# Softplus in a selective scan: in three of eight rounds one plus the exponential is made by ScalarE, and VectorE adds the positive part before the correction

## The reference

```
proj = u @ x_proj_w                                   # u: 2048 x 384
dt   = softplus(proj[..., :12] @ dt_w + dt_b)         # for each of two directions
B, C = proj[..., 12:28], proj[..., 28:]
h    = exp(dt * A) * h + (dt * u) * B                 # over the tokens, 16 states a channel
y    = sum over the states of h * C
```

## Time and profile before

| | us |
|---|---|
| median of 3 runs | 908.35 (907.75 to 909.34) |
| the profiled execution | 906.87 |
| its span on the core | 905.1 |

### The profile page before, as it was taken

The page is one execution under the profiler, slowest core; times in us unless marked ns, Lnnn a source line. Parts: engine busy times, 40 slices in busy tenths (PEclk is TensorE's granted clock), DMA queues, the critical chain, the costliest instruction groups (busy, mean ns, idle before and its releaser), DMA issues.

```text
span 905.1 us, 16651 instructions
## 1 busy us (share of the span) xinstructions
PE 779.2 (86%) x6060; PEld 705.2 (78%) x6061; DVE 733.4 (81%) x874; ACT 645.0 (71%) x1258; POOL 534.6 (59%) x343
## 2 busy tenths in 40 slices
PE   0389776899998999989999899995966899999990
PEld 0133335899998999989999899995955899999990
DVE  3788899889999899998999999998949455555554
ACT  0365879999999999989999999991331444444421
POOL 6430003799997999969999799893000344444420
PEclk9999989999999999999999999997955899999996
DMA  5003103265574764644746567377350111111106
GB/s 87 3 35 106 9 27 119 65 160 176 125 199 148 175 216 121 173 157 122 199 120 161 175 159 194 127 152 247 109 197 8 41 43 43 43 43 43 43 23 217
DMA packets 46453, 104.43 MB, mean 115 GB/s; under 512 B 16448, under 2 KB 25176, under 8 KB 46392
## 3 DMA queue, kind: packets, MB, share of 16 engines
q1 hardware_dynamic: 35784, 74.67, 25.5%
q0 software_dynamic: 8352, 27.07, 15.0%
q10 hardware_dynamic: 2256, 1.87, 0.6%
HBM read 83.77 MB, written 19.82 MB: 114 GB/s over the span
## 4 chain that ended last, share of the span: by engine, by line
PE 47%; DVE 22%; ACT 17%; POOL 7%; issue 4%; DMA 2%; DVEq 0%; ACTq 0%; POOLq 0%; SPq 0%
PE ps L1434 15%; PE ps L1738 8%; PE ps L1556 8%; DVE arena L836 8%; ACT arena L1261 6%; PE ps L1721 6%; POOL arena L623 5%; ACT arena L1244 5%; PE ps L1726 4%; ACT arena L1247 3%; PE ps L1454 3%; PE ps L1457 1%; DVE stats L670 1%; DVE arena L793 1%; DVE arena L802 1%
## 5 line engine op out<-in xcount | busy, mean ns | idle before, releaser
L623 POOL TENSOR_TENSOR arena<-arena 128x1024 f32<-128x1024 f32 x192 | 395.1, 2283 | 121.2 <-DVE arena L836 117.8
L836 DVE TENSOR_TENSOR_SCAN arena<-arena,ps 128x1024 f32<-128x1024 f32 x192 | 426.3, 2277 | 21.3 <-PE ps L1556 16.9
L1434 PE MATMUL ps<-ident,arena 128*128 128x128 f32 (+3 forms) x2622 | 347.2, 279 | 80.4 <-ACT arena L1124 37.4
L1434 PEld LDWEIGHTS ps<-ident,arena 128*128 128x128 f32 (+3 forms) x2622 | 298.1, 143 | 101.5 <-issue 52.9
L1261 ACT ACTIVATE arena<-arena,neg_a 128x510 f32<-128x510 f32 x384 | 241.0, 708 | 0.1
L627 POOL DMA_INDIRECT arena<-x_rows,arena x39 | 37.7, 967 | 160.5 <-DVE arena L1020 79.7
L1556 PE MATMUL ps<-arena,ln_in 128*128 128x128 f32 x768 | 104.0, 280 | 0.0
L1556 PE MATMUL ps<-arena 128*128 128x128 f32 x768 | 101.4, 275 | 0.0
L1556 PEld LDWEIGHTS ps<-arena,ln_in 128*128 128x128 f32 x768 | 95.9, 196 | 0.0
L1556 PEld LDWEIGHTS ps<-arena 128*128 128x128 f32 x768 | 93.3, 192 | 0.0
L1738 PE MATMUL ps<-arena,ln_in 128*128 x468 | 82.7, 327 | 0.8 <-DVE arena L1051 0.8
(11 more groups left out here) (217 smaller groups left out, 883.7 us busy)
## 6 DMA issues: line engine op xcount, KB each, us to landing
arena<-b_rows SPq DMA_DIRECT2D x64, 512.0 KB, 3.8
arena<-ws SPq DMA_DIRECT2D x16, 576.0 KB, 6.1
arena<-wf POOLq DMA_DIRECT2D x16, 576.0 KB, 7.9
arena<-hf POOLq DMA_DIRECT2D x16, 576.0 KB, 7.4
summed_first<-arena SPq DMA_DIRECT2D x8, 576.0 KB, 5.4
summed_second<-arena SPq DMA_DIRECT2D x8, 576.0 KB, 7.7
arena<-summed_second SPq DMA_DIRECT2D x8, 576.0 KB, 5.9
gates_dram<-arena SPq DMA_DIRECT2D x4, 768.0 KB, 3.4
```

The costliest lines, as they stand in the source:

```text
L623: g_.tensor_tensor(state[i % STATES], state[i % STATES], c_bc[u % C_BUFS], ALU.mult).then_inc(s_mul, 1)
L836: v.tensor_tensor_scan(o, a, x, 0.0, ALU.mult, ALU.add).then_inc(s_scan, 1)
L1434: return mm(o, src, ident[at:at + parts, at:at + parts], start=start, stop=True, is_transpose=True, skip_group_check=True)
```

## The change

In rounds 1, 3 and 5 ACT makes w = 1 + e, with a new instruction (Identity with a bias of 1, 128x1536) right behind the logarithm, and sets a new semaphore `s_w`; DVE leaves its own addition out there. In the same rounds DVE takes the positive part first (it waits for `s_l`), then the correction (it waits for `s_e` and `s_w`), then the subtraction. Rounds 0, 2, 4, 6 and 7 are as before. The function `pos_log` is cut in two, `add_pos` and `subtract_correction`.

```diff
--- before.py
+++ after.py
@@ -333,6 +333,7 @@
         s_e = sem("softplus_exp_ready")
         s_c = sem("softplus_corr_ready")
         s_pl = sem("softplus_pos_and_log_added")
+        s_w = sem("softplus_one_plus_exp_ready")
         s_l = sem("softplus_log_ready")
         s_lb_ps = sem("dt_and_b_product")
         s_lb = sem("dt_and_b_rows_ready")
@@ -418,6 +419,7 @@
         s_passed = sem("waits_passed")
         FRONT_LOADS, PAR_LOADS = 2, 34
         DT_BANK = 2
+        BY_ACT = (1, 3, 5)
         FIRST_BANKS = (0, 0, 0, 1, 0, 1, 0, 1)
 
         c_rows = b_rows
@@ -789,10 +791,13 @@
 
                 w, e = sp_w[n % SP], sp_e[n % SP]
                 dve.wait_ge(s_e, n + 1)
-                st.then(v.tensor_scalar(w, e, 1.0, None, ALU.add))
+                if n in BY_ACT:
+                    dve.wait_ge(s_w, BY_ACT.index(n) + 1)
+                else:
+                    st.then(v.tensor_scalar(w, e, 1.0, None, ALU.add))
                 v.scalar_tensor_tensor(w, w, -1.0, e, ALU.add, ALU.subtract).then_inc(s_c, 1)
 
-            def pos_log(n):
+            def add_pos(n):
 
                 g, d = divmod(n, 2)
                 dt = dt_all[g][d]
@@ -800,6 +805,10 @@
                 bank = ps[:, DT_BANK + DB * d:DT_BANK + DB * (d + 1), :].rearrange("p a b -> p (a b)")
                 flat = dt.rearrange("p a b -> p (a b)")
                 v.scalar_tensor_tensor(flat, bank, 0.0, flat, ALU.max, ALU.add).then_inc(s_pl, 1)
+
+            def subtract_correction(n):
+                g, d = divmod(n, 2)
+                dt = dt_all[g][d]
                 dve.wait_ge(s_pl, n + 1)
                 dve.wait_ge(s_c, n + 1)
                 v.tensor_tensor(dt, dt, sp_w[n % SP], ALU.subtract).then_inc(s_dt, 1)
@@ -808,12 +817,18 @@
                 v.tensor_tensor(dtu_b if d else dtu, dt_all[0][d], u_all[0], ALU.mult).then_inc(s_dtu, 1)
 
             for n in range(2 * NG):
-                correction(n)
+                if n in BY_ACT:
+                    add_pos(n)
+                    correction(n)
+                else:
+                    correction(n)
                 if n == 0:
                     dve.wait_ge(s_rset, 1)
                     st.then(v.tensor_copy(gain_1[:], ps[:, 1, 0:E]))
                     v.tensor_copy(w_route_sb[:, :, E + DR + 1:RC], ps[0:KC, 1, E:(1 + KT) * E].rearrange("p (k e) -> p k e", k=KT)).then_inc(s_wr, 1)
-                pos_log(n)
+                if n not in BY_ACT:
+                    add_pos(n)
+                subtract_correction(n)
                 if n in (4, 5):
                     dve.wait_ge(s_dt, n - 3)
                     times_u(n - 4)
@@ -1223,6 +1238,8 @@
                             keep_first_dtu_t(1)
                     act.wait_ge(s_e, n + 1)
                     a.activation(dt, sp_e[n % SP], ACT.Ln, bias=1.0).then_inc(s_l, 1)
+                    if n in BY_ACT:
+                        a.activation(sp_w[n % SP], sp_e[n % SP], ACT.Identity, bias=1.0).then_inc(s_w, 1)
                     if d == 0 and g + 1 < NG:
                         keep_lb(g + 1)
                     elif d == 0:
```

## The result

Measured with the prediction: 903.16 us (median of 4, 902.70 to 904.36) against 908.85 (median of 4, 907.75 to 909.37), ratio 0.9946 with a 95% interval of 0.9934 to 0.9958. I had forecast 904.6, 3.8 less than before; the medians differ by 5.7. Two more comparisons of the same two kernels gave 0.9971 (0.9961 to 0.9980) and 0.9964 (0.9950 to 0.9977), so 0.29% and 0.36% after 0.54%. The forecast of 904.6 thus lies 1.4 above the first median. By that comparison's 5.7 us the result falls into the case to which I had given 0.02 (more than 4.6); by the 3.0 and 3.5 us of the two later ones it falls into the second and the first case.

A forecast was written before the change was run, and what follows sets the result against it. Two engines in a row bound the softplus stage: DVE releases PE's banks, PE feeds ACT, ACT starts the loop. DVE's end 2.64 us and ACT 4.3 earlier start the loop 3.8 earlier: 908.35 - 3.8 = 904.6 us, range 902.9 to 907.2.

The forecast's parts named there:

- the case to which I had given 0.02: Whole kernel: an advance of more than 4.6 us, chance 0.02.
- the second and the first case: Second: only DVE's addition cut arrives, advance 1.6 to 3.3 us, chance 0.22; first: advance 3.3 to 4.6, chance 0.56.
- DVE's own cut: DVE's softplus stage: three additions fewer, less a new wait of 0.3 in round 1, end it 2.64 us earlier.
- The bank of round 5 free 4.32 earlier: DVE's positive part of round 5, moved to the front, ends at 126.94 instead of 131.26 us, releasing PE's bank.
- Identity 1.48, between 1.48 and 1.65: ACT's new 128x1536 instruction: duration taken as 1.48 us, at most 1.65.
- Exponential of round 4 1.8 earlier, of round 7 4.3 earlier: ACT in the softplus stage: round 4's exponential starts at 115.7 us, round 7's at 132.1 instead of 136.38.
- PE: the product of round 7 starts near 127 and at full clock: Expected profile sign on PE: round 7's product starts near 127 us, formerly 131.30, at full clock.
- The loop starts 3.8 earlier: ACT's copy behind item 1's blocks comes at 145.3 instead of 149.13 us, an advance of 3.8.
- All behind it moves as a block: From the copy ACT has the chain to 177 us; weights' scaling and all behind it shift together by 3.8.
- Only DVE's cut: Rival: PE stays slow, ACT comes late, the loop starts only about 2.6 us earlier: 905.7 us; chance 0.22.
- Given back later: Rival: the program behind the stage loses 2 to 3 us at PE's varying clock: 906.6 to 908.4; chance 0.15.
- ACT as the bound: Rival: added work on ACT makes the kernel slower, 910.0 to 911.8 us, if an Identity costs over 2.8; chance 0.05.

The follow-up runs named there:

- positive part first in round 7: Changed kernel with the positive part first in round 7 too, that round's addition left on DVE; run twice: 905.04 us (ratio 0.9961) and 904.71 us (0.9957).
- the order alone: Against the kernel before: positive part first in rounds 1, 3 and 5, additions stay on DVE, ACT gets nothing; 908.10 us against 908.10, ratio 1.0000.
- PE kept busy: Changed kernel with positive part first in round 7 too, plus 20 useless 128x128 matmuls (filler) in PE's idle times; 903.25 us, ratio 0.9950.
- each Identity twice: Changed kernel with each Identity on ACT made twice in a row; 908.29 us, ratio 1.0001; the changed kernel had 905.11 on the same chip.
- POOL in rounds 1, 3, 5: Changed kernel with one plus the exponential of rounds 1, 3 and 5 made by POOL (GpSimd) instead of ACT; 911.18 us against 908.46, ratio 1.0036.
- the move alone: Against the kernel before: ACT makes the additions of rounds 1, 3 and 5, DVE keeps its old order; 908.65 us against 908.10, ratio 1.0005.
- round 7 too: Changed kernel with round 7 treated as rounds 1, 3 and 5: positive part first, Identity on ACT; 906.51 us against 908.46, ratio 0.9983.
- POOL in rounds 1 to 7: Changed kernel with additions of rounds 1 to 7 on POOL (GpSimd), positive part first in all of them; 917.41 us against 908.46, ratio 1.0115.

## Why the prediction was right, point by point

*DVE's own cut, 0.98 a round less 0.3 once: 2.64.* Measured 2.49 (first scan at S + 50.25 for 52.74). The wait cost 0.29 from start to start (1.97 for 1.68), as counted. The waited step from correction to subtraction takes 1.85, not the 1.78 of the step from positive part to subtraction, so the cut is 0.93 a round and not 0.98.

*The bank of round 5 free 4.32 earlier.* Measured 4.2 (end of the positive part at S + 32.76 for 36.98). As counted, the logarithm was there in rounds 3 and 5: DVE has no new wait in them.

*Identity 1.48, between 1.48 and 1.65.* 1.472.

*Exponential of round 4 1.8 earlier, of round 7 4.3 earlier.* 1.81 and 4.09. The second lacks the 0.38 that ACT still waited for PE: there the step "PE: the product of round 7 starts near 127 and at full clock" failed. The start was right (126.84), the clock was 0.53, although PE had been idle for 1.12 only; I had taken a short gap for a sure sign of the full clock. It cost little, since ACT was nearly the bound: 0.38 of wait. Other runs have the full clock at the same place, the two with the positive part first in round 7, the order alone and the one with PE kept busy (2.84 each).

*The loop starts 3.8 earlier.* The copy came 3.3 to 3.8 earlier (against both profiles of before), the scaling 3.3 to 3.75.

*All behind it moves as a block.* The end of the loop did, by 3.4 to 3.7, but not for the reason given. From DVE's first scan to the end of the loop it is 472.6 and 472.7 in the two profiles of before, and 471.5 to 471.7 in the three of the changed kernel; with PE kept busy it is 471.3, though ACT is 1.7 to 2.1 further ahead there. So 2.5 of the gain is DVE's earlier end, some 1.1 is ACT no longer being late behind it (its decays let DVE's fourth scan wait 1.41 before and 0.20 now), and beyond that an earlier ACT brings nothing. My sum had put all of it on ACT's side, with ACT as what starts the loop and DVE's scan moving along; that step of the sum was wrong, and that its 3.8 lies so near to the 3.4 to 3.7 is partly luck.

The experiments bear the division out. Take the time from the first scan to the end of the loop. Where the scaling comes at most 26.5 us behind the first scan, this time is the short one of the changed kernel: 471.7 with each Identity twice and 471.5 with POOL in rounds 1, 3, 5, though DVE's end is 2.5 and 6.4 later there. Where it comes 27.1 or more behind, as in both profiles of before, it is 472.6 to 473.2: the order alone, the move alone, round 7 too. Two profiles don't fit: 472.3 with the scaling only 25.5 behind, in the first of the two with the positive part first in round 7 (471.4 in the second), and 470.7 with POOL in rounds 1 to 7.

*The rivals.* Only DVE's cut: the move alone has that cut in work and gains nothing, so the cut needs the order to arrive; with the order DVE's end gives 2.5 of the 3.4 to 3.7, so this rival, to which I had given 0.22, had hold of the larger part, and what it lacked is the 1.1 on ACT. Given back later: not seen; rest and loop are the same. ACT as the bound: not at 1.47 an Identity. I had given 2.8 us each as the point from which the kernel gets slower; with 3.0 each the gain is gone by the medians (ratio 1.0001), while the trace still has the end of the loop 0.9 earlier than before; so the point is near 3 or somewhat above it.

What stays open: why the first comparison shows 2 us more than the stage holds, by what the filler's 1.5 us in the medians would come, if it is real, and why S and the stretch behind the loop (284.9 to 287.7 in all profiles) differ from one execution to the next by as much as the gain is in doubt.

## What to carry to other kernels

Where two engines work in a row, ask of an instruction that is to move from the fuller to the emptier one whether the order of the rest leaves time for it; here the move alone and the order alone gave nothing, and both together the whole gain: put what needs nothing of it (and frees someone else's buffer) in front. Count the cover on the receiving engine in its waits, and expect them to shrink with the move. Judge a fraction of a per cent by distances between fixed points of several traces as well as by the medians.

## What the runs showed of the hardware

- An engine idle in the profile isn't free: POOL's addition of 128x1536 took 4.07 to 5.68 us (DVE 0.95, ACT 1.47), and DVE's two-input instructions beside it took up to 4.76 instead of 1.76. The two take turns: every one of the eight DVE instructions with both inputs in the arena that began while POOL worked ended 0.73 or 0.74 behind POOL's end, and POOL's additions took 4.07 to 4.08 except for the four that began when such a DVE instruction had 1.2 us or more still to run (5.23 to 5.68); it kept its own 1.76. All seven additions of the run with rounds 1 to 7 on POOL, from the view of that line:

```profile
L604 POOL TENSOR_SCALAR arena<-arena x7: 4073/4084/5241, 100.2 to 146.3; 128x1536 f32<-128x1536 f32 x7
```

- PE's granted clock at the product of round 7 differs between runs with the same gaps in front of it. In all three profiles of the changed kernel it was at the low level (4.53 to 4.54 us for the product) behind idle times of 0.56 and 1.12 with half a microsecond of work between; in the second run with the positive part first in round 7 the same idle times stood there, and the product took 2.84; so it did in the run with the order alone. First the second profile of the changed kernel, then that second run:

```profile
127.42 4.54 PE L1543 MATMUL ps<-arena 128*128 128x512 f32 x6 [1.12 <-DVE arena L807]
```

```profile
128.50 2.84 PE L1544 MATMUL ps<-arena 128*128 128x512 f32 x6 [1.12 <-DVE arena L808]
```

  So the last gap alone doesn't decide it. With 20 small matmuls in the gaps the clock stayed at 1.00 through both products, but was 0.64 on average in 132 to 140 us all the same.
- A waited step on DVE behind a two-input instruction in the arena took 1.85 from start to start, behind one with an input in PSUM 1.78, unwaited ones 1.66 to 1.68.
